# Attention logits with tokens on the partitions: row tiles of 64x128, scale in the keys, mask by an opening matmul

## The reference, cut to what matters

```python
xn = rmsnorm(layernorm(x));  mn = rmsnorm(ctx)
q = rope(einsum('BTD,NDH->BTNH', xn, q_w), positions S..S+T) * HEAD_DIM ** -0.5
k, v = kv_w applied to mn;   k = rope(k)
logits = einsum('BTKGH,BSKH->BKGTS', q, k)
masked = where(mem_mask, logits, -2.3819763e+38)
probs = softmax(masked, axis=-1)                 # over 64 context rows
x = x + tanh(g_xattn) * (probs @ v) @ out_w
x = x + tanh(g_ffn) * experts(layernorm(x))      # second stage, not touched by the change
```

## Time and profile before

| what | value |
|---|---|
| median of 3 runs | 1729.66 us (1722.69 to 1732.41) |
| the profiled execution: time, span | 1737.22 us, 1735.4 us |
| TensorE matmul, weight load | 93%, 65% busy |
| VectorE, ScalarE, GpSimd | 75%, 43%, 50% busy |
| the chain that ended last | 60% TensorE, 13% DMA, 13% VectorE, 7% issue |
| mean granted TensorE clock | 0.984 |

### The profile page before, as it was taken

One profiled execution on the slowest core, in us unless ns is written; L12 is line 12 of the kernel. 1 busy time (PEld: TensorE's weight loads), 2 busy tenths in 40 slices (PEclk: granted clock), 3 DMA queues, 4 the chain that ended last, 5 costly groups with the idle time before them and its releaser, 6 DMA issues.

```text
span 1735.4 us, 51613 instructions
## 1 busy us (share of the span) xinstructions
PE 1608.4 (93%) x22424; PEld 1134.3 (65%) x22424; DVE 1303.7 (75%) x1893; ACT 737.6 (43%) x966; POOL 859.6 (50%) x1020
## 2 busy tenths in 40 slices
PE   8899999999999999999888889999898989899885
PEld 4677777777777777777676555666555566555662
DVE  5777777777777777777748767778777777776776
ACT  3532323233323232333234555555555455555453
POOL 4468777877787778777731233132233122233112
PEclk9999999999999999999999999999999999999998
DMA  7634545454554445545474888877888777888766
GB/s 290 176 100 152 191 128 180 158 167 153 160 184 159 160 157 158 178 141 180 159 229 155 214 210 222 229 213 204 217 217 227 213 212 203 222 212 213 206 183 167
DMA packets 182705, 325.31 MB, mean 187 GB/s; under 512 B 23120, under 2 KB 35280, under 8 KB 181072
## 3 DMA queue, kind: packets, MB, share of 16 engines
q1 hardware_dynamic: 137216, 239.15, 42.9%
q0 software_dynamic: 17616, 32.52, 11.5%
q10 hardware_dynamic: 27648, 50.34, 8.9%
HBM read 243.23 MB, written 78.71 MB: 186 GB/s over the span
## 4 chain that ended last, share of the span: by engine, by line
PE 60%; DMA 13%; DVE 13%; issue 7%; ACT 4%; POOL 3%; ACTq 1%; SPq 0%; DVEq 0%; POOLq 0%
PE ps L1498 13%; PE ps L959 11%; PE ps L1006 10%; PE ps L1468 7%; DMA gat<-in_W 6%; PE ps L1019 5%; DMA xin<-out 4%; PE ps L974 3%; DMA out<-xin 3%; PE ps L1032 3%; DVE mx L738 2%; PE ps L993 2%; ACT lg L705 2%; POOL xin L184 1%; DVE res L1394 1%
## 5 line engine op out<-in xcount | busy, mean ns | idle before, releaser
L184 POOL TENSOR_SCALAR xin<-xin,r_all,nb_all 128x512 f32<-128x512 f32 x128 | 116.0, 911 | 529.2 <-DMA xin<-out 375.6
L1394 DVE STREAM_TRANSPOSE res<-res 128x2048 f32<-128x2048 f32 x128 | 292.1, 2295 | 0.1
L1348 ACT ACTIVATE gat<-ps 128x1536 f32<-128x1536 f32 (+1 forms) x128 | 171.0, 1344 | 224.9 <-PE ps L1468 224.6
L959 PE MATMUL ps<-xTh,qh 128*128 128x512 f32 x512 | 210.2, 411 | 5.5 <-DVE qs L755 2.0
L1412 DVE COPY res<-ps 128x1024 f32<-128x1024 f32 x128 | 156.5, 1224 | 60.7 <-PE ps L1522 60.5
L959 PE MATMUL ps<-xTh,ql 128*128 128x512 f32 x512 | 201.2, 393 | 0.0
L959 PE MATMUL ps<-xTl,qh 128*128 128x512 f32 x512 | 200.4, 392 | 0.0
L1468 PE MATMUL ps<-sel,xin 32*128 32x128 f32 x4096 | 156.4, 287 | 42.4 <-issue 13.4
L1400 DVE COPY gat<-ps 128x512 f32<-128x512 f32 (+1 forms) x128 | 104.0, 815 | 92.8 <-PE ps L1468 92.4
L1468 PEld LDWEIGHTS ps<-sel,xin 32*128 32x128 f32 x4096 | 133.0, 190 | 57.3 <-issue 32.0
L1358 ACT ACTIVATE res<-ps 128x1024 f32<-128x1024 f32 x128 | 130.9, 1024 | 85.6 <-PE ps L1522 85.6
(11 more groups left out here) (174 smaller groups left out, 3303.3 us busy)
## 6 DMA issues: line engine op xcount, KB each, us to landing
gat<-in_W ACTq DMA_DIRECT2D x192, 256.0 KB, 6.0
xT<-in_xT SPq DMA_DIRECT2D x32, 1024.0 KB, 6.1
xin<-in_x SPq DMA_DIRECT2D x64, 512.0 KB, 3.7
out<-xin SPq DMA_DIRECT2D x64, 512.0 KB, 4.0
xin<-out SPq DMA_DIRECT2D x128, 256.0 KB, 4.2
xin<-in_W SPq DMA_DIRECT2D x128, 256.0 KB, 4.1
out<-xin POOLq DMA_DIRECT2D x120, 256.0 KB, 7.7
xT<-in_W SPq DMA_DIRECT2D x68, 256.0 KB, 4.4
```

The source lines that it names most:

```text
L184: e.tensor_scalar(self.xn[:, t, :], self.xn[:, t, :], self.r[:, i, t:t + 1], self.nb[:, i, t:t + 1], ALU.mult, ALU.add).then_inc(self.m_xn ...
L959: last = e.matmul(ps[:, 2 + n % 2, :], a[:, c, n * DH:(n + 1) * DH], b[:, c, :], start=(k == 0), stop=(k == len(parts) - 1))
L1348: e.activation(o, v, ACT.Copy).then_inc(m_gaA.sem, 1)
L1394: e.transpose(v, v).then_inc(m_tr.sem, 1)
```

## The change

What it does, for each unit:

- `logits(u)` puts tokens on the partitions at once. The queries `qc` are stationary (64 rows of one head half, 128 tokens), the keys `kb` stream with 64 columns. Rows 0 to 63 write bank 0, rows 64 to 127 bank 1. That is 32 matmuls with row tiles of 64x128 instead of 8 with tiles of 64x64.
- Ahead of them two bf16 matmuls of 512 columns open the two banks with the mask: a row of ones `onerow` (stationary) against `fillb` (streaming).
- ScalarE's step `logits` (L630) and TensorE's `logits_T` (L986) go. `top_of` reads banks 0 and 1 in a strided view and waits for the logits themselves (`m_L`).
- `queries` for n < 2 no longer waits for ScalarE's emptying; `probs_T` gains a wait for the subtraction; `logits(u)` waits for `probs_lo` of the unit before; the key loads wait for `m_L`.
- The order of heads in the probabilities changes, and `vraw` and `out_wT` with it.

In the prologue: `mask` is loaded to all partitions as 1024 bytes each, two VectorE passes over 1024 elements and one small one make `fillb` and `onerow`; GpSimd makes `rdiag` (1024 elements); TensorE makes the key scales with eight matmuls into bank 3 ahead of the product k = 2; ScalarE takes them out into `qs`; GpSimd multiplies the keys by them in two passes (`scaled_keys`), and the key transfers wait for that. `kscale`'s two small VectorE steps and two transfers go. The buffer `lt` goes, and what used it early moves to `qc` and `lg`.

```diff
             def logits(u):
 
                 b = u // 2
-                e.wait_ge(d_kb[b % 2].sem, d_kb[b % 2].at(b // 2))
-                for k in range(2):
-                    e.wait_ge(m_rot.sem, m_rot.at(u, 2 + k))
-                    for p in range(2):
-                        for h in range(2):
-                            r, o = slice(h * S, (h + 1) * S), slice((h ^ p) * S, ((h ^ p) + 1) * S)
-                            last = e.matmul(ps[o, 3 + p, :], kb[r, b % 2, k * S:(k + 1) * S], qc[r, 2 * p + k, :],
-                                            start=(k == 0), stop=(k == 1))
-                last.then_inc(m_L.sem, 1)
-
-            def logits_T(u, tp):
-                e.wait_ge(m_lt.sem, m_lt.at(u))
                 if u:
-                    e.wait_ge(m_pl.sem, m_pl.at(u - 1, tp))
+                    e.wait_ge(m_pl.sem, m_pl.at(u - 1, 1))
                 else:
                     e.wait_ge(m_vce.sem, m_vce.at(0, NC - 1))
-                for t in range(2):
-                    for p in range(2):
-                        last = e.transpose(ps[:, tp, (2 * t + p) * P:(2 * t + p + 1) * P],
-                                           lt[:, p, (2 * tp + t) * P:(2 * tp + t + 1) * P], ident[:])
-                last.then_inc(m_LT.sem, 1)
+                    e.wait_ge(m_fill.sem, m_fill.at(0, 1))
+                for h in range(2):
+                    r = slice(h * S, (h + 1) * S)
+                    e.matmul(ps[:, h, :].rearrange("p (g s) -> p g s", s=S), onerow[r, :], fillb[r, b:b + 1, :].broadcast_to([S, 8, S]),
+                             start=True, stop=False, skip_group_check=True)
+                e.wait_ge(d_kb[b % 2].sem, d_kb[b % 2].at(b // 2))
+                for p in range(2):
+                    e.wait_ge(m_rot.sem, m_rot.at(u, 2 * p + 1))
+                    for t in range(TH):
+                        for k in range(2):
+                            for h in range(2):
+                                r, o = slice(h * S, (h + 1) * S), (2 * t + p) * S
+                                last = e.matmul(ps[:, h, o:o + S], qc[r, 2 * p + k, t * P:(t + 1) * P], kb[r, b % 2, k * S:(k + 1) * S],
+                                                start=False, stop=(k == 1), skip_group_check=True)
+                last.then_inc(m_L.sem, 1)
...
             def top_of(u, tp):
-                e.wait_ge(m_LT.sem, m_LT.at(u, tp))
-                e.tensor_reduce(out=mx[:, tp, :], in_=heads(ps[:, tp, :]), op=ALU.max, axis=AX_X).then_inc(m_mx.sem, 1)
+                v = ps[:, 0:2, tp * 4 * S:(tp + 1) * 4 * S].rearrange("p h (g s) -> p h g s", s=S)
+                top = mx[:, tp, :].rearrange("p (h g) -> p h g", h=2)
+                e.wait_ge(m_L.sem, m_L.at(u))
+                e.tensor_reduce(out=top, in_=v, op=ALU.max, axis=AX_X).then_inc(m_mx.sem, 1)
...
-                if unit(g + 1):
-                    logits(g + 1)
...
             for g in range(-1, NU):
-                if unit(g):
-                    logits_T(g, 0)
-                    logits_T(g, 1)
                 if unit(g + 1):
                     for n in range(3):
                         queries(g + 1, n)
...
+            def scaled_keys(k):
+
+                v = kr[:, :, k * S:(k + 1) * S]
+                e.wait_ge(m_kr.sem, m_kr.at(0, k))
+                e.wait_ge(m_scc.sem, m_scc.at(0))
+                e.tensor_tensor(v, v, kscale, ALU.mult).then_inc(m_krx.sem, 1)
...
+                    e.wait_ge(m_vTl.sem, m_vTl.at(0, 1))
+                    e.wait_ge(m_dg.sem, m_dg.at(0))
+                    for o in range(2):
+                        for m in range(NC // 2):
+                            last = e.matmul(ps[o * S:(o + 1) * S, 3, m * P:(m + 1) * P], ones[:], rdiag[:, o * NC // 2 + m, :],
+                                            start=True, stop=True, skip_group_check=True)
+                    last.then_inc(m_scl.sem, 1)
```

More of the change, by code:

```diff
@@ L234, in attention @@
     b1s, b2s, part, rowk = consts[1:5]
+    NC = B * S // P
     st = ExitStack()
@@ L247, in attention @@
         wcl = sb("wcl", [P, C, E], F32R)
-        lt = sb("lt", [P, 2, HT])
+        fillb = sb("fill", [P, B, S], BF16)
+        onerow = sb("onerow", [P, P], BF16)
+        kb = sb("kb", [P, 2, 2 * S])
+        mx = sb("mx", [P, 2, 8])
+        sm = sb("sm", [P, 2, 8])
+        rc = sb("rc", [P, 2, 8])
+        va, r1, vb, vc, r2, sc = (sb(n, [P, RING, TH]) for n in ("va", "r1", "vb", "vc", "r2", "sc"))
+        cst = sb("cst", [P, NC, 6])
         lx2, lx3 = sb("lx2", [P, HT]), sb("lx3", [P, HT])
@@ L307, in attention @@
         gr = sb("gr", [P, NC])
-        kscale = sb("kscale", [P, 2, NC])
+        ones = sb("ones", [P, S])
         mean_of = qs[:, 0, 0:P]
+        kscale = qs[:, 1, :].rearrange("p (b s) -> p b s", s=S)
+        rdiag = qs[:, 2:4, :].rearrange("p a s -> p (a s)").rearrange("p (j k) -> p j k", k=P)
         rrow = pr_[:, 0, :]
@@ L405, in sync @@
             e.dma_start(gts[:, 1:2], gf_in.partition_broadcast(P)).then_inc(d_small.sem, 16)
-            e.dma_start(mk[0:S, :], mask).then_inc(d_small.sem, 16)
-            e.dma_start(mk[S:P, :], mask).then_inc(d_small.sem, 16)
+            e.dma_start(mk[:], mask.rearrange("b s -> (b s)").partition_broadcast(P)).then_inc(d_small.sem, 16)
             e.dma_start(ident[:], ident_in).then_inc(d_small.sem, 16)
@@ L568, in gpsimd @@
                 lo(0, c)
+                if c in (1, 2):
+                    scaled_keys(c - 1)
             norm_scale(0)
@@ L814, in vector @@
                 e.tensor_scalar(v, v, rs1[:, c:c + 1], None, ALU.mult).then_inc(m_qsc.sem, 1)
-            e.wait_ge(d_small.sem, d_small.at(0, 4))
-            e.tensor_copy(mkf[:], mk[:]).then_inc(m_mkf.sem, 1)
+            e.wait_ge(d_small.sem, d_small.at(0, 3))
+            e.tensor_copy(mkf, mk[:]).then_inc(m_mkf.sem, 1)
             e.wait_ge(m_mkf.sem, m_mkf.at(0))
-            e.tensor_scalar(fill[:], mkf[:], -FILL, FILL, ALU.mult, ALU.add).then_inc(m_fill.sem, 1)
+            e.tensor_scalar(fillb[:].rearrange("p b s -> p (b s)"), mkf, -FILL, FILL, ALU.mult, ALU.add).then_inc(m_fill.sem, 1)
+            first_of = lambda h: ident[:, h * S:h * S + 1].broadcast_to([P, P])
+            e.tensor_tensor(onerow[:], first_of(0), first_of(1), ALU.add).then_inc(m_fill.sem, 1)
             for h in range(2):
@@ L834, in vector @@
             values_lo(1)
[L835 to L838, removed]
             nk = HT // S
@@ L990, in probs_T @@
+                last.then_inc(m_L.sem, 1)
             def probs_T(u, tp):
+                e.wait_ge(m_sb.sem, m_sb.at(u, 1))
                 e.wait_ge(m_pr.sem, m_pr.at(u, tp))
-                for k in range(4):
-                    last = e.transpose(ps[:, tp, k * P:(k + 1) * P], pr_[:, tp, k * P:(k + 1) * P], ident[:])
+                for h in range(2):
+                    for t in range(2):
+                        last = e.transpose(ps[:, tp, (2 * t + h) * P:(2 * t + h + 1) * P], pr_[:, tp, (2 * h + t) * P:(2 * h + t + 1) * P], ident[:])
@@ L1608 @@
     ow = np.asarray(L0_xattn_out_w).transpose(1, 0, 2)
-    owT = np.asarray(L0_xattn_out_w)[[0, 3, 1, 2]].transpose(2, 0, 1).reshape(C, P, H * DH).transpose(1, 0, 2).reshape(P, C * H * DH)
+    owT = np.asarray(L0_xattn_out_w).transpose(2, 0, 1).reshape(C, P, H * DH).transpose(1, 0, 2).reshape(P, C * H * DH)
     arrays = {
         "x": x, "xT": np.asarray(x).transpose(0, 2, 1), "ctx_1024": ctx_1024, "ctxT": np.asarray(ctx_1024).transpose(2, 0, 1).reshape(D, B * S),
-        "mask": np.asarray(mask_BxS2_bk0).T, "g_xattn": g_xattn, "g_ffn": g_ffn,
+        "mask": np.asarray(mask_BxS2_bk0), "g_xattn": g_xattn, "g_ffn": g_ffn,
         "rms": np.asarray(L0_xattn_rms_scale).reshape(C, P).T, "q_w": qp, "kv_w": kv, "out_w": ow, "out_wT": owT,
```

67 lines of the change are left out of this document (28 added, 39 removed).

## The result

The changed kernel takes 1807.38 us (median; 1804.11 to 1812.82) against 1731.04 us of the kernel before on the same chips: ratio 1.0449, 95% interval 1.0398 to 1.0500, slower by 76 us. A second comparison gave 1819.17 against 1730.55, ratio 1.0508 (1.0470 to 1.0547). The profiled execution took 1809.92 us, 72.7 more than that of before.

A forecast was written before the change was run, and what follows sets the result against it. Each unit was taken as a ring of 6.5 us of VectorE and 18.4 us of TensorE. Logits and mask, +58.6 us over 31 units, plus prologue, +3.0, added 61.6 to 1729.66: 1791 us, range 1738 to 1806.

The forecast's parts named there:

- The experts unchanged in length: Stage after the attention loop: expected to keep its length, with the loop beginning 3 us later.
- The block of logits: TensorE's logits in each unit of the attention loop: from 1.88 us to 3.55 + 0.22 = 3.77.
- The choice of L1468 over L1498: Trace row pricing a round of logits: 0.111 us by L1468 (128-column loads), not 0.058 by L1498 (64-column loads).
- the mask's opener: Two new bf16 matmuls of 512 columns, side by side, in each unit: about 0.22 us.
- cheap loads: Rival for the logits block: the stream sets the pace, 0.058 us a round, +9.2 us, 1739 us; chance 11%.
- in between: Rival for the logits block: a load hides in part, 0.08 us a round, +31 us, 1761 us; chance 14%.
- dear loads: Rival for the logits block: load and stream of one tile follow each other, 5.2 us, +113, 1842 us; chance 6%.
- The transposes saved 0: Removing the logits' transposes, 0.79 us a unit inside VectorE's part: saves 0, TensorE's wait at L959 grows to about 1.07.
- A unit: One round of the attention loop: +1.89 us, from 24.9 to 26.8 us; 31 x 1.89 = +58.6 us.
- Unit 0: First unit of the attention loop: block followed at once by top_of, without ScalarE's step and transposes, so costs about nothing.
- The prologue: Work ahead of the attention loop, TensorE's key scales and VectorE's mask passes: +3.0 us, ends +1 and +5.
- The main case: The whole kernel at 1780 to 1800 us, with the prologue's ends and a load between 0.105 and 0.113; chance 64%.

The follow-up runs named there:

- a_half: The changed kernel with one of the two halves of the head width left out of the logits; 1737.77 us.
- a_load64: The changed kernel with the weight loads of the logits cut from 128 to 64 columns, streams unaltered; 1759.72 us.
- a_stream32: The changed kernel with streams of 32 columns instead of 64 in the logits, loads of 128 columns unaltered; 1851.42 us, a single execution.
- b_behind_2604: The kernel before with 2604 added matmuls of one column behind everything on TensorE; 1812.02 us with the tail taken off.
- b_code_behind: The kernel before with 1302 added matmuls of one column behind everything on TensorE; 1770.99 us with the tail taken off, two executions.
- b_order: The kernel before with part_of_x(g + 1) ahead of the third query tile and VectorE's statistics ahead of turned(g + 1, 2); 1713.93 us, ratio 0.9933.
- b_code_84: The kernel before with 84 added matmuls of one column a unit in the attention loop, 2604 in all; 1815.03 us.

## Why the prediction was wrong

It said 1791 us within 1738 to 1806; the median is 1807.38. Sign and mechanism held, and the sum for the stage that the change touches was met, 61.6 us against 61.2 measured. Point by point:

- **"The experts unchanged in length"** is the step that failed. It was stated, not costed: an unaltered stage was taken as an unaltered time, a term of zero without a reason. The runs showed a longer experts part in its place: by 11.5 us in the profiled execution, 15 by the medians (76.3 less 61.2; the interval of the ratio gives 8 to 25), 27 in the second comparison. a_half, with half of the logits' matmuls left out, is without it, but it doesn't grow in proportion to added matmuls; transfers of weights land later in these programs, and whether that or something else lengthens the stage stays open. Without it the kernel would stand at 1731 + 61 = 1792.
- **The block of logits.** Taken as 3.55 + 0.22 = 3.77; measured 3.84. The choice of L1468 over L1498 as the nearest row was right, and a_load64 and a_stream32 show for what reason: the load of 128 columns sets the pace, at 0.112 us a round, with 64 or 32 columns streaming beneath. The row itself says 0.34 / 3 = 0.113, of which the prediction took 0.111; 32 x 0.113 + 0.22 would have been 3.84. The 0.22 of the mask's opener was right as well, by the distances of starts. The rule of the Trainium skill, page "TensorE: Matmul & The Clock Gate", section "LDWEIGHTS (loading the stationary operand)", columns over 1.2 per ns, gives an estimate of 107 ns for a load of 128 columns and 53 for 64; measured were 112 and 63 a round, the second with a stream as wide as the load. The rival of cheap loads is out, as are those in between and of dear loads.
- **The transposes saved 0**, as said, and TensorE's wait grew from 0.28 to 1.18 us (1.07 forecast). Two experiments moved them in and out at no cost.
- **A unit** grew by 1.90 us for 1.89. The block grew by 1.96; other steps of TensorE are each about 0.02 shorter, which nobody forecast.
- **Unit 0** was put at nothing, with `top_of` as what follows at once. From its last rotation to its first maximum it gained 1.0 us (2.1 for 3.1, since ScalarE's step and the transposes are gone). The next distance, 27.2 us, is 0.45 longer than the others, because TensorE's queries waited for GpSimd's low parts, a queue that the step of unit 0 didn't name.
- **The prologue** came out at 2.9 us (its last rotation ends at 85.87 for 82.94) for 3.0. Together: 2.9 less 1.0, 2.35 for the first distance and 30 x 1.90 make 61.2. That this meets the sum to half a microsecond is partly luck: among the kernels whose loop is as before, a traced first gather stands anywhere from 876.1 (b_behind_2604) to 879.2 us (b_code_behind).
- **Range and chances.** The main case was put at 1780 to 1800 and the range ended 6 us above it, with no room for the stage that makes up half of the time. Executions of the kernel before alone lie between 1719 and 1741 us.

## What to carry to other kernels

When small matmuls replace large ones, count the columns loaded as well as those streamed, and price the round by the row of the trace that has the same load; swapping which operand is stationary doubled this block without changing one product. A step that leaves TensorE is worth nothing while another engine's part of the ring covers it, and the same wait tells what to move there: work that needs nothing of that part, together with the steps that would next stand in its way, gave 0.7% (b_order) where the removal of the transposes gave none. And a stage isn't a constant of the sum because its code is unaltered; leave room for it in the range.

## What the runs showed of the hardware

- A round of two row tiles of 64x128 with fp32 loads of 128 columns costs 0.11 us: 3.52 us by the chain (3.61 from start to start) for 32 rounds with streams of 64 columns, 3.49 with streams of 32; with loads of 64 columns 2.01 by the chain.
- TensorE's clock fell to 1.2 GHz around the end of a block of loads with streams of 32 columns (3.5 us long, the engine never idle in it) in 23 of 31 units, and not after the same block with streams of 64. The values behind then took up to 5.4 us instead of 3.0. In b_code_84 it fell in 13 of 31 units behind 84 matmuls of one column (2.08 us), again with no idle time, and in none behind 42 of them.
- Programs with 672 to 2688 more small matmuls, in the loop or behind everything, came with transfers of weights that land in 4.9 to 5.1 us instead of 4.4 to 4.6. By the median their experts stage was 8 to 28 us longer, but in single traces it was not always so; the relation to the number isn't steady, that the one causes the other isn't shown, and the cause stays open.
